# Attention units in another order: projections from step 0, the last two groups' value products one step sooner

## The reference

```python
qkv = jnp.einsum('bse,ehd->bshd', x, w_qkv)
q, k, v = jnp.split(qkv, 3, axis=-1)
logits = jnp.einsum('bqhd,bkhd->bhqk', q, k) / sqrt(64)
probs = softmax(where(tril, logits, neg), axis=-1)
out = jnp.einsum('bshd,hde->bse', jnp.einsum('bhqk,bkhd->bqhd', probs, v), w_out)
```

## Time and profile before

| | us |
|---|---|
| median of 3 runs | 3183.21 (3181.66 to 3183.53) |
| the profiled execution, its own time | 3178.04 |
| its span, first to last instruction | 3175.8 |
| PE busy, share of the span | 3040.6, 96% |
| DVE busy | 2185.1, 69% |
| ACT busy | 1710.6, 54% |
| POOL busy | 1606.0, 51% |
| PE's granted clock, mean | 0.985 |

### The profile page before, as it was taken

The page is one execution under the profiler, slowest core; times in us unless marked ns, Lnnn a source line. Parts: engine busy times, 40 slices in busy tenths (PEclk is TensorE's granted clock), DMA queues, the critical chain, the costliest instruction groups (busy, mean ns, idle before and its releaser), DMA issues.

```text
span 3175.8 us, 64704 instructions
## 1 busy us (share of the span) xinstructions
PE 3040.6 (96%) x22707; PEld 2412.5 (76%) x22707; DVE 2185.1 (69%) x5088; ACT 1710.6 (54%) x3866; POOL 1606.0 (51%) x2380
## 2 busy tenths in 40 slices
PE   5599999999999999999999999999999999999998
PEld 3489998999977777777777777777777777777776
DVE  6844444444337777887787787778777777877776
ACT  3454444445435555555555555555555555555554
POOL 2132221222116666666666666666666666666664
PEclk7799999999999999999999999999999999999999
DMA  6122221222113334334333423433342343334222
GB/s 212 34 79 78 72 70 46 75 78 72 59 59 74 82 96 108 74 85 108 91 82 93 111 74 81 112 91 81 91 114 74 79 110 94 77 90 115 71 72 70
DMA packets 204433, 272.60 MB, mean 86 GB/s; under 512 B 61264, under 2 KB 161616, under 8 KB 204128
## 3 DMA queue, kind: packets, MB, share of 16 engines
q1 hardware_dynamic: 179712, 201.94, 23.8%
q0 software_dynamic: 24416, 66.65, 8.0%
HBM read 102.80 MB, written 33.55 MB: 43 GB/s over the span
## 4 chain that ended last, share of the span: by engine, by line
PE 60%; ACT 4%; issue 4%; DVE 2%; SPq 0%; DMA 0%; DVEq 0%; ACTq 0%
PE S L1275 15%; PE O L1312 13%; PE T L1288 10%; PE W L1191 9%; PE S L1191 3%; PE W L1206 3%; PE S L1206 3%; ACT pr L1350 3%; PE W L1226 3%; PE S L1226 2%; ACT pT L1342 1%; DVE pr L1406 1%; SPq L1130 0%; PE S L1214 0%; DMA pT<-squares 0%
## 5 line engine op out<-in xcount | busy, mean ns | idle before, releaser
L1350 ACT ACTIVATE pr<-pr,negm 128x128 f32<-128x128 f32 (+7 forms) x1024 | 787.3, 770 | 670.0 <-DVE negm L1406 665.7
L1551 POOL TENSOR_SCALAR pr<-pr,rinv 128x128 f32<-128x128 f32 (+7 forms) x1024 | 755.5, 745 | 427.4 <-DVE rinv L1412 424.6
L1406 DVE CUSTOM_DVE_ANT_0 pr<-S,late 128x128 f32<-128x128 f32 (+7 forms) x1024 | 730.4, 750 | 40.0 <-PE S L1275 23.7
L1312 PE MATMUL O<-pT,vv 128*64 128x256 f32 (+1 forms) x5120 | 556.1, 364 | 3.1 <-DMA pT<-squares 2.7
L1312 PEld LDWEIGHTS O<-pT,vv 128*64 128x64 f32 x5120 | 346.2, 137 | 205.0 <-issue 45.1
L1288 PE MATMUL T<-ident,pr 128*128 128x128 f32 x2718 | 425.2, 281 | 32.7 <-DVE pT L1342 18.0
L886 DVE TENSOR_TENSOR hl<-h,hh 128x512 fp32r<-128x512 f32 x256 | 190.2, 744 | 323.3 <-ACT hh L847 318.3
L1288 PEld LDWEIGHTS T<-ident,pr 128*128 128x128 f32 x2718 | 297.8, 141 | 140.0 <-issue 118.7
L1342 DVE COPY pT<-T 128x512 f32<-128x512 f32 (+3 forms) x644 | 305.1, 498 | 143.0 <-PE O L1312 111.5
L843 ACT ACTIVATE h<-pH,b1c 128x512 f32<-128x512 f32 x256 | 175.8, 687 | 365.2 <-PE pH L773 353.5
L1275 PE MATMUL S<-kh,qh 64*128 64x512 f32 (+2 forms) x1536 | 317.0, 409 | 6.6 <-DVE negm L1406 6.4
(11 more groups left out here) (193 smaller groups left out, 6590.2 us busy)
## 6 DMA issues: line engine op xcount, KB each, us to landing
pT<-squares SPq DMA_DIRECT2D x756, 128.0 KB
pT<-squares POOLq DMA_DIRECT2D x252, 128.0 KB
y<-yb SPq DMA_DIRECT2D x128, 128.0 KB, 1.7
wr<-in_L_attn_w_qkv SPq DMA_DIRECT2D x128, 128.0 KB, 2.3
x<-in_L_attn_x SPq DMA_DIRECT2D x16, 512.0 KB, 5.3
xn<-xn SPq DMA_DIRECT2D x16, 512.0 KB, 5.2
w1r<-in_L_ffn_w SPq DMA_DIRECT2D x8, 1024.0 KB
w2r<-in_L_ffn_w SPq DMA_DIRECT2D x8, 1024.0 KB
```

Of the source, the lines that this page charges most:

```text
L1312: ins = e.matmul(O[hs, a:GQ], vv[n // 2 % 2][:, kt, vs], turned_p, start=(kt == 0), stop=(kt == KT - 1))
L1350: e.activation(pr[i][:, 0:w], pr[i][:, 0:w], ACT.Exp, bias=negm[:, i:i + 1], scale=-1.0, accum_out=rsum[:, i:i + 1]).then_inc(expd.sem, 1)
L1406: e.tensor_tensor_reduce(pr[i][:, 0:w], S[s % 2][:, off:off + w], late[:, SEQ - w:], 1.0, -MASKED, ALU.add, ALU.min, negm[:, i:i + 1]).the ...
L1551: e.tensor_scalar(pr[i][:, 0:width(s)], pr[i][:, 0:width(s)], rinv[:, i:i + 1], 1.0, ALU.mult, ALU.mult).then_inc(scaled.sem, 1)
```

## The change

The edit changes tables and constants only; no operation is added or taken away.

```diff
-    KEPT_BY_ACT = {1, 10, 11, 12, 14, 15} | set(range(CHUNKS, FIRST_CH[STEPS], 2))
+    KEPT_BY_ACT = {1, 4, 5, 10, 11, 14} | set(range(CHUNKS, FIRST_CH[STEPS], 2))
...
-    STEP_OF = {'v0': 0, 'p0': 2, 'o1': 4, 'o2': 5, 'xn': 5, 'p1': 6, 'v1': 6, 'p2': 7, 'p3': 9, 'o3': 12, 'o0': 14}
-    BANK_OF = {'p0': 2, 'p1': 0, 'p2': 2, 'p3': 2, 'o2': 2, 'xn': 0, 'v0': 2, 'o3': 2, 'v1': 1, 'o0': 2, 'o1': 1}
+    STEP_OF = {'p0': 0, 'o1': 1, 'p1': 1, 'xn': 3, 'v0': 4, 'v1': 4, 'o2': 6, 'p2': 6, 'p3': 9, 'o3': 12, 'o0': 14}
+    BANK_OF = {'p0': 0, 'p1': 2, 'p2': 2, 'p3': 2, 'o2': 0, 'xn': 1, 'v0': 0, 'o3': 2, 'v1': 1, 'o0': 2, 'o1': 1}
...
-    POOL_AT = {'place0': 0, 'place1': 5, 'fetch0': 2, 'fetch1': 5, 'weigh': 6, 'add': 7, 'total': 14, 'split_w': 13, 'split_wv': 10}
+    POOL_AT = {'place0': 4, 'place1': 4, 'fetch0': 2, 'fetch1': 2, 'weigh': 9, 'add': 14, 'total': 14, 'split_w': 13, 'split_wv': 13}
...
-        SQUARE_LAG = 4
+        SQUARE_LAG = 3
...
-        AFTER = [13, 14, 19, 27]
+        AFTER = [13, 14, 18, 26]
```

## The result

The changed kernel takes 3261.6 us (median of 4 runs, 3252.9 to 3267.0) against 3182.4 for the kernel before, run beside it: 1.025 of it, with a 95% interval of 1.0224 to 1.0277. The forecast was 3194 us, with a range up to 3214. The sign was right; the size was not: 79 us were lost where 11 were forecast. The profiled execution of the changed kernel is the longest of its four, 3267.0 us.

The account below looks back on a forecast made before the run. PE, busy 96% of the span, was taken as the bound. PE gaps 2.5, V3's waits for the placing DMAs 8.3 and the last unit 0.4 summed to 11 us: median 3183.2 becomes 3194, range 3172 to 3214.

Parts of the forecast that it names:

- The last square ends: DVE's last square transpose, after which the placing DMAs may start: 0.9 us later, at 9.3 after S0 instead of 8.41.
- V3 is ready: On PE, V3, which waits for the sixteen placing DMAs, starts at 21.35 us after S0 in place of 21.75.
- the cover: Time from last square transpose to V3: 13.34 us becomes 12.0, 1.3 shorter.
- T9 and T10: PE's two waits per unit, 0.28 us for DVE's chunk 8 and 0.18 for ACT's chunk 10, stay: 0 gained.
- rival 3: DVE or POOL reach T11 or p0 0.3 us late: 16 us on top of 11, 3210; chance 0.13.
- rival 4: DVE's first square and POOL's weights' split shut each other out, p0 waits 0.9: 55 us on top, 3249; chance 0.03.
- the semaphore comes with the end of that thin traffic, within 0.1 us: Ahead of V3, the placing DMAs' go-ahead follows the last DMA traffic within 0.1 us, read from the unit at 1509.29.
- the sum had 8.3: V3's waits for the placing DMAs with 1.3 us less cover: 7.1 us in 55 units, 8.3 in 64.
- the share near 1 says that the engines are the limit, so I cost this at 0: POOL's four placing DMAs go out later, at about 14 to 16; SP's twelve end later still: cost 0.
- could cost 1 us a unit: Reserve, kept in the high end: DMA engines idle early for want of POOL's share, 1 us a unit.
- Gaps on PE: Gaps where PE changes kinds of work: +0.04 us a unit, 2.5 us in all; range -0.1 to +0.15 a unit.
- the 0.15 us around 34.82: Test of the sum: a unit without a DMA wait should be within 0.15 us of 34.82.

Follow-up runs that it names:

- e1: Changed kernel with POOL's placing DMAs back at steps 0 and 5, no longer all four at step 4: 3215.3 us, 1.011 of the kernel before.
- e13: Changed kernel with both fetches of y moved from step 2 to step 5, behind POOL's placing DMAs: 3229.6 us, 1.016 of the kernel before.
- e2: Kernel before with only POOL's four placing DMAs moved from steps 0 and 5 to step 4: 3185.4 us, ratio 1.001.
- e3: Changed kernel with V3 one place back (26 to 27), so T5 is ahead of it again: 3233.6 us, 1.017 of the kernel before.
- e6: Kernel before with only V3 one place sooner (27 to 26), three transposes earlier: 3190.5 us, ratio 1.003.
- e12: Kernel before with only V3 two places sooner (27 to 25), POOL's DMAs untouched: 3324.0 us, ratio 1.045.

## Why the prediction was wrong, by its own steps

**Right.** The last square ends 9.14 after S0 (forecast 9.3), V3 is ready at 21.15 (21.35), the cover is 12.0 (12.0). T9 and T10 wait as before (0 gained). There is no wait at T11 and none at p0, so rival 3 and rival 4 did not come; POOL's rates stayed. That V3 waits, and that this decides, was the forecast's mechanism. Nothing behind V3 made the waits up.

**Wrong, the largest: "the semaphore comes with the end of that thin traffic, within 0.1 us".** It rested on one unit, at 1509.29, and on taking the thin traffic there for the placing DMAs. SP's queue in that unit:

```profile
1495.83 9.38 SPq L1130 DMA_DIRECT2D pT<-squares  x12
1505.25 0.58 SPq L1134 DMA_DIRECT2D out<-res  x1
```

Behind the twelve, SP issues a store of finished output. By the packet records the last placing packet ended at 1508.73; what still ran up to V3 are packets of 1 KB on SP's queue, those of a DMA behind the twelve, and the store is the only one issued there. The last semaphore update came at 1509.24 and V3 0.05 later: in this very unit the lag was 0.51 us. In none of 61 units of the kernel before is it under 0.3. With the measured lag the margins of the kernel before give 22.9 us of waits for 1.35 us less cover; the sum had 8.3. So this term was mis-sized by 15 us, and e1, which has it nearly alone, shows 33.7 with 10 from POOL's second pair (issued at 6.4 in place of 5.2). The Trainium skill (DMA: Bandwidth & Descriptors, "Anatomy of one DMA") puts a DMA's fixed time of about 2 us mostly behind the last byte; I had set the rule aside by that unit. The section describes DMAs issued by GpSimd, and twelve of these sixteen are SP's. By the runs it has the direction right, and its 2 us, laid onto the end of the traffic, are about four times what is measured.

**Wrong: "the share near 1 says that the engines are the limit, so I cost this at 0".** The share near 1 was read in a kernel in which POOL's queue ran beside SP's from the start. With SP's twelve and the fetches, but without POOL's four, the mean share in the third to fifth us after the last square of the changed kernel is 0.90, 0.74, 0.81, against 1.01, 1.04, 1.01 before, and the placing DMAs land 0.93 us later. e1 shows that POOL's first two are the cause: with them back the share is 1.04, 1.03, 0.99. Why SP alone falls short is known in part only. Its first eleven issues start 0.56 to 0.66 us apart, most of them 0.63 (medians; 128 KB each, 207 GB/s), against 222 GB/s at a share of 1.00 (the window above): by my estimate this pace can feed a share of 0.93. The 0.74 and 0.81 lie below that while SP issues at the same pace; the fetches, issued 1.8 and 3.2 us after the last square in the unit shown, fall there, but in e13, where they come later, it is 0.82 and 0.78. That stays open. The Trainium skill (DMA: Bandwidth & Descriptors, "Issuing engines are not separate DMA queues") says that several issuing engines save only sequencer time, usually small beside the DMA; here what POOL's early pair saved was not small. The text's own reserve, "could cost 1 us a unit", was the right figure, but it went into the high end in place of the sum. It is 37 us of waits (e1). That both fetches now stood ahead of the four was in the order of POOL's rows, and was not priced.

**Missing.** What waits bring with them: 11.2 us at a lower granted clock, and the 7.1 us of waits for xnt. The price of adding the two parts up: the late share alone costs 3.5 us (e2), the rest of the change without most of it 33 us (e1), both together 79 to 86, since beyond the margin each 0.1 us is paid in 62 units.

**Gaps on PE: +0.04 us a unit forecast, -0.12 measured.** The cut of the transposes around V3 costs 0.12 to 0.15 (e3, e6), more than the 0.08 allowed, so that the rest of the new order saves about 0.25, where -0.04 was forecast. Which join it comes from was not taken apart. A unit without a wait ahead of V3 would take 34.21 + 0.46 = 34.67 us, at the very edge of the 0.15 us around 34.82 that the prediction allowed itself.

## What to carry to other kernels

A wait that is hidden by a narrow margin is priced by the distribution of that margin over all units, and the margin is taken from the semaphore's update, not from the end of traffic. A share of traffic has no owner: before it is read as the end of one transfer, look at what else was issued on the queues. When a change shortens the cover from one side and delays the transfers from the other, the two are summed before they are compared with the margin, and every instruction newly ahead of a DMA issue on its queue counts. A full DMA share says that the present queues together fill the engines, not that one of them would do it alone.

## What the chip showed that I had not expected

- From the end of the last placing packet to the last semaphore update: 0.47 us on average (0.27 to 0.84) in the changed kernel, 0.54 (0.31 to 0.92) in the one before, 0.55 in e12, 0.69 in e1; from there to the start of the waiting instruction 0.04. Transfers of 128 KB within the chip's own memory, sixteen at once.
- One queue with twelve such transfers held the DMA engines at 0.74 to 0.90 of their time; SP's and POOL's together held them at 1.0. SP issues one every 0.63 us, which explains a part of it.
- After a wait of PE of about 2 us in an otherwise busy stretch the granted clock went to 0.50 (1.2 GHz) for some 3 us, about when PE had begun again or shortly after: 1.4 to 1.7 us lost each time, in seven units of the changed kernel; five other waits of 1.80 to 2.19 us were not followed by it.
- Four DMA issues on POOL cost it 2.1 us of its own time (0.52 each), and a fetch with indices 1.0 us plus a gap of 0.3.
